# A gated cross-attention layer on one core: the loads of the split queries requested by SyncE in place of ScalarE, with other buffers and another front

## The reference

```
x = x + tanh(g_xattn) * xattn(layernorm(x), ctx)     # 16 heads of 32
x = x + tanh(g_ffn)   * ffn(layernorm(x))
xattn: q = x Wq + bq;  k = y Wk + bk;  v = y Wv + bv
       out = softmax(q k^T / sqrt(32)) v;  return out Wo + bo
ffn:   s = max(amax(|x|), 1e-6)/127;  x_q = clip(round(x / s))
       return (x_q @ weight_q^T) * s * weight_scale + bias
```

## Time and profile before

| what | before |
|---|---|
| median of 3 timed executions | 806.0 us (805.67 to 806.8) |
| the profiled execution: device time | 809.15 us |
| the profiled execution: span of the profile | 807.0 us |
| mean granted TensorE clock | 0.991 of full speed |
| busy: PE, PEld | 769.5 us (95%), 531.2 us (66%) |
| busy: DVE, ACT, POOL | 584.6 us (72%), 610.1 us (76%), 533.8 us (66%) |
| DMA | 183.21 MB, mean 227 GB/s |

### The profile page before, as it was taken

The page is one execution under the profiler, slowest core; times in us unless marked ns, Lnnn a source line. Parts: engine busy times, 40 slices in busy tenths (PEclk is TensorE's granted clock), DMA queues, the critical chain, the costliest instruction groups (busy, mean ns, idle before and its releaser), DMA issues.

```text
span 807.0 us, 16228 instructions
## 1 busy us (share of the span) xinstructions
PE 769.5 (95%) x5835; PEld 531.2 (66%) x5890; DVE 584.6 (72%) x879; ACT 610.1 (76%) x844; POOL 533.8 (66%) x524
## 2 busy tenths in 40 slices
PE   9896999999999999999999999999999989999996
PEld 6664467667666766766676676667667657666563
DVE  5864778677776857777686777768578796756568
ACT  5774668778687877868788786878778677787785
POOL 4836348485775948577595857759485765855588
PEclk9998999999999999999999999999999999999998
DMA  8899897879888887878878798788879757746722
GB/s 284 298 311 247 212 272 212 248 212 261 239 225 246 222 265 211 258 227 236 251 225 235 216 258 250 219 248 228 251 218 264 213 161 242 208 151 185 202 67 104
DMA packets 119519, 183.21 MB, mean 227 GB/s; under 512 B 37648, under 2 KB 47248, under 8 KB 117392
## 3 DMA queue, kind: packets, MB, share of 16 engines
q1 hardware_dynamic: 92368, 133.33, 54.2%
q10 hardware_dynamic: 27072, 48.84, 23.6%
HBM read 123.91 MB, written 58.22 MB: 226 GB/s over the span
## 4 chain that ended last, share of the span: by engine, by line
PE 75%; DVE 7%; DMA 6%; issue 5%; POOL 3%; ACT 3%; SPq 1%; ACTq 1%; DVEq 0%; POOLq 0%
PE bank_b L437 25%; PE bank_a L437 15%; PE scores L492 7%; PE scores L511 6%; PE sum_ps L519 6%; PE pv_ps L523 6%; PE bank_a L567 4%; DMA q_rows<-q_parts 2%; DVE row_max L1228 2%; PE scores L437 1%; PE bank_a L542 1%; PE bank_b L567 1%; DMA q_stack<-q_rows 1%; DMA x_in<-in_x 1%; SPq L232 1%
## 5 line engine op out<-in xcount | busy, mean ns | idle before, releaser
L1584 POOL TENSOR_TENSOR o_lo<-on,o_hi 128x512 fp32r<-128x512 f32 x48 | 64.6, 1346 | 135.9 <-ACT o_hi L907 135.9
L1228 DVE TENSOR_REDUCE row_max<-scores 128x16 f32<-128x1920 f32 x64 | 137.7, 2151 | 10.3 <-PE scores L492 10.3
L1239 DVE TENSOR_TENSOR q_parts<-q_sb,q_parts 128x512 fp32r<-128x512 f32 x60 | 64.3, 1072 | 111.4 <-ACT q_parts L851 111.4
L889 ACT ACTIVATE probs<-scores 120x2048 f32<-120x2048 f32 x64 | 120.0, 1876 | 18.8 <-PE scores L511 18.6
L1540 POOL TENSOR_TENSOR xt<-xt,rstd_b 128x512 f32<-128x512 f32 x60 | 97.8, 1665 | 6.8 <-DMA xt<-in_x_t 5.8
L492 PEld LDWEIGHTS scores<-k_sb,q_sb 32*128 32x128 f32 x1984 | 61.0, 186 | 51.9 <-issue 44.4
L1580 POOL TENSOR_TENSOR x<-x,gbo_r 128x512 f32<-128x512 f32 x64 | 93.6, 1474 | 0.6 <-DMA x<-in_x 0.5
L1592 POOL TENSOR_TENSOR x<-x,gbias_r 128x512 f32<-128x512 f32 x64 | 83.2, 1302 | 15.7 <-ACT cen L913 14.7
L511 PE MATMUL scores<-q_stack,k_stack 128*120 128x512 f32 x256 | 73.0, 406 | 12.5 <-DVE row_max L1228 8.7
L1597 POOL TENSOR_TENSOR x<-x,u_sb 128x512 f32<-128x512 f32 x56 | 74.2, 1324 | 7.1 <-DVE u_sb L1320 7.0
L437 PE MATMUL bank_b<-xt_hi,wq_hi 128*128 128x512 f32 x188 | 77.0, 409 | 1.2 <-DVE xt_lo L1218 1.2
(11 more groups left out here) (235 smaller groups left out, 1927.5 us busy)
## 6 DMA issues: line engine op xcount, KB each, us to landing
q_stack<-q_rows ACTq DMA_DIRECT2D x183, 256.0 KB, 4.3
q_rows<-q_parts SPq DMA_DIRECT2D x61, 512.0 KB, 4.5
xt<-in_x_t SPq DMA_DIRECT2D x16, 1024.0 KB, 8.7
x<-in_x SPq DMA_DIRECT2D x64, 256.0 KB, 4.2
out_x<-x SPq DMA_DIRECT2D x61, 256.0 KB, 2.3
x_in<-in_x SPq DMA_DIRECT2D x60, 256.0 KB, 5.1
k_stack<-k_rows SPq DMA_DIRECT2D x96, 120.0 KB, 4.4
k_rows<-k_parts SPq DMA_DIRECT2D x28, 240.0 KB, 2.2
```

Source lines behind the costliest of these rows:

```text
L889: act.activation(probs[0:KEYS], scores[0:KEYS], ACT.Exp, scale=SCALE).then_inc(p_ready, 1)
L1228: dve.tensor_reduce(row_max[:].rearrange("p (t r) j -> p r t j", r=ROWG)[:, :, :, j], scores[:, :, 0:QT * KEYS].rearrange("p r (t k) -> p ...
L1584: pool.tensor_tensor(o_lo[i % 2][j], on[:], o_hi[i % 2][j].bitcast(F32), ALU.subtract).then_inc(o_split, 1)
```

## The change

SP requests all `stack_q` loads; ACT requests none of them. `q_sb` becomes one buffer and `q_parts` two. DVE's `split_low` takes the query from the PSUM bank, adds the bias in the same instruction and subtracts the high part, so `q_sb` is free earlier, and the bank later: PE now waits for `q_split` before it writes a bank again. The low parts of the keys move from DVE to POOL. `split_high` waits for the store of two groups before. In step 0 SP requests the stack of group 3 and the store of the queries of batch 1, group 1, ahead of the loads for batch 2; in the front POOL and SP have another order, and ACT's conversion of the output weights stands behind `split_high(1, 1)`. At the end of step 14 the maxima are transposed ahead of the last chunk of an output projection. `max_sp` is stored with overlapping windows.

```diff
-        q_sb = [sb(f"q_sb{i}", [P, S]) for i in range(2)]
-        q_parts, k_parts = sb("q_parts", [P, 2, S], F32R), sb("k_parts", [P, 2, KEYS2], F32R)
+        q_sb = sb("q_sb", [P, S])
+        q_parts = [sb(f"q_parts{i}", [P, 2, S], F32R) for i in range(2)]
+        k_parts = sb("k_parts", [P, 2, KEYS2], F32R)
...
@@ block.sync @@
             store_rstd(2)
-            load_rstd(2)
-            load_xt(2)
 
             def step(i):
+                if i > 0:
+                    stack_q(i, 2)
                 if is_batch(e):
                     store(e, 0)
...
+                stack_q(i, 3)
                 if is_batch(e):
                     store(e, 1)
                 if is_batch(b):
                     store_q(b, 1)
                 if i == 0:
+                    load_rstd(2)
+                    load_xt(2)
                     load_x(f, 2)
...
+                if is_batch(b):
+                    stack_q(b, 0)
                 if is_batch(k_of(i)):
                     store_k(k_of(i) // 2, 2 * (i % 2))
...
+                if is_batch(b):
+                    stack_q(b, 1)
@@ block.tensor @@
                     pe.wait_ge(v_ready, nth(b, 1))
+                if keys_next or values_next and i > 1 or not is_batch(n):
+                    pe.wait_ge(q_split, nth(b - 1, DT, 0))
                 if is_batch(e):
                     quantised_layer(e, 1, bank_a if is_batch(n) else bank_b)
...
                     quantised_layer(e, 3, bank_b)
+                pe.wait_ge(q_split, nth(b - 1, DT, 2))
@@ block.scalar @@
             def split_high(n, j):
                 act.wait_ge(q_ready, nth(n, DT, j))
...
-                if n == 1 and j == 0:
-                    act.wait_ge(q_stored[0], stores_of(0, 0))
-                elif n > 0:
-                    act.wait_ge(q_stored[(j - 1) % DT], stores_of(n - (j == 0), (j - 1) % DT))
-                act.activation(q_parts_of(n, j)[0], q_of(n, j), ACT.Copy).then_inc(q_hi_done, 1)
-
-            def stack_q(n, j):
-                act.wait_ge(q_stored[j], stores_of(n, j))
-                act.wait_ge(s_done, nth(n, DT, j) - 2)
-                for block, part in enumerate((0, 1, 0)):
-                    load(q_stacked[j % 2], q_stack[j % 2][STRIPS[block]].bitcast(F32),
-                         q_rows[j, part].rearrange("(r d) s -> d r s", d=DH))
+                if n > 0 and j >= 2:
+                    act.wait_ge(q_stored[j - 2], stores_of(n))
+                if n == 1 and j < 2:
+                    act.wait_ge(q_stored[j], stores_of(0))
+                if n > 1 and j < 2:
+                    act.wait_ge(q_stored[j + 2], stores_of(n - 1))
+                act.activation(q_parts_of(n, j)[:, 0], q_of(n, j), ACT.Copy).then_inc(q_hi_done, 1)
@@ block.vector @@
-            def split_low(n, j):
+            def split_low(n, j, bank):
                 dve.wait_ge(q_hi_done, nth(n, DT, j))
-                dve.tensor_tensor(q_parts[:, 1], q_of(n, j), q_parts[:, 0].bitcast(F32), ALU.subtract).then_inc(q_split, 1)
+                parts = q_parts_of(n, j)
+                dve.scalar_tensor_tensor(out=parts[:, 1], in0=bank[:], scalar=bq_c[:, j:j + 1], in1=parts[:, 0].bitcast(F32),
+                                         op0=ALU.add, op1=ALU.subtract).then_inc(q_split, 1)
@@ block.gpsimd @@
                 if is_batch(e):
                     add_out(e, 2)
+                if is_batch(k_of(i)):
+                    low_k(k_of(i) // 2, 2 * (i % 2))
                 if is_batch(m):
                     x1_deviations(m, 0)
```

More of the change, by code:

```diff
@@ L202, in q_parts_of @@
         def q_parts_of(n, j):
[L203 to L206, removed]
+            return [o_lo1, o_hi1][j - 2][:, 0:2] if n == 0 and j >= 2 else q_parts[j % 2][:]
         def k_parts_of(pair, j):
@@ L278, in store_q @@
                     sp.wait_ge(q_stacked[j % 2], 48 * nth(n - 1, 2, j // 2))
[L279 to L284, removed]
+                sp.dma_start(q_rows[j].rearrange("h p s -> p h s"), q_parts_of(n, j).bitcast(F32)).then_inc(q_stored[j], 16)
             def stack_q(n, j):
-                sp.wait_ge(q_stored[j], stores_of(n, j))
+                sp.wait_ge(q_stored[j], stores_of(n))
                 if n > 0 or j >= 2:
@@ L294, in store_k @@
             def store_k(pair, j):
[L295 to L298, removed]
+                sp.wait_ge(k_split, nth(pair, DT, j))
                 if pair > 1:
@@ L335, in _ @@
             load_ctx(1)
+            store_k(0, 0)
+            store_q(0, 0)
             load_x(2, 0)
-            store_k(0, 0)
             store_k(0, 1)
-            store_q(0, 0)
+            stack_q(0, 0)
             load_x(2, 1)
             stack_k(0, 0)
-            stack_q(0, 0)
             store_q(0, 1)
+            load(rest_landed, u_sb[:].bitcast(I32), rows(wq8))
+            stack_q(0, 1)
+            load_x(2, 2)
+            store_q(0, 2)
+            load_x(2, 3)
             store_k(0, 2)
             store_k(0, 3)
[L346 to L349, removed]
             store_q(0, 3)
-            load_x(2, 2)
-            load_x(2, 3)
             load(rest_landed, gbo_r[:], bo.partition_broadcast(P))
@@ L499, in turn_max @@
                 for t in range(QT):
-                    ins = pe.matmul(bank[:, t * P:(t + 1) * P], max_sp[:, t], ident_r[:], start=True, stop=True)
+                    ins = pe.matmul(bank[:, t * P:(t + 1) * P], max_sp[:, t * DH:t * DH + P], ident_r[:], start=True, stop=True)
                 ins.then_inc(max_turned, 1)
@@ L679, in step @@
                     quantised_layer(m, 0, bank_a)
+                pe.wait_ge(q_split, nth(b - 1, DT, 3))
+                if is_batch(m) and i < LAST - 1:
                     project_o(m, 3, bank_b)
+                if i == LAST - 1:
+                    for c in range(DT - 1):
+                        add_heads(m, 3, c, bank_b)
                 if i == 0:
@@ L997, in step @@
                     split_high(b, 1)
-                stack_q(i, 3)
+                if i == 0:
+                    act.wait_ge(wo_gated, 1)
+                    act.activation(flat(wo_hi), flat(wo_stage), ACT.Copy).then_inc(wo_hi_done, 1)
                 log_sums(i, 1)
@@ L1336, in step @@
                 if is_batch(b):
-                    split_low(b, 0)
+                    split_low(b, 0, bank_b)
                 if is_batch(e):
@@ L1353, in step @@
                 if is_batch(b):
-                    split_low(b, 1)
+                    split_low(b, 1, bank_b)
                     maxima(b, 1)
@@ L1374, in step @@
                 if is_batch(b):
-                    split_low(b, 2)
+                    split_low(b, 2, bank_a)
                     maxima(b, 2)
```

88 lines of the change are left out of this document (43 added, 45 removed).

## The result

The changed kernel takes 817.06 us (median of 4 runs, 812.8 to 818.28) beside 806.4 for the kernel before on the same chip (805.67 to 807.0). The ratio, taken over the single executions and not from the two medians, is 1.0123, with a 95% interval of 1.0084 to 1.0162. Forecast were 795.5 us and a range of 789 to 803. The profiled execution takes 816.25 us, its span 814.6, beside 809.15 and 807.0.

The account below looks back on a forecast made before the run. PE was taken to bound the kernel from step 2 on, waits the front. From the median: 806.0 - 12.4 (front) + 3.6 (PE's new waits) - 1.1 (low part) - 0.6 (step 14) = 795.5 us; range 789 to 803.

Parts of the forecast that it names:

- The front's gains: Steps 0 and 1: 6.2 third quarter, 1.2 fourth, 2.3 first, 1.5 step 1, 1.2 shorter maxima waits; 12.4 us in all.
- The third quarter's 9.3 us: Step 0, third quarter: 9.3 us long instead of 15.44, 6.2 less, with bounds of 3 and 6.3.
- the first quarter's lower bound: Step 0, first quarter: gain of 0 instead of 2.3 us if the later keys' stack takes over PE's wait.
- I take 1.2, with 0 and 2.0 as bounds: Step 0, fourth quarter: 1.2 us gained from a higher granted clock after less idle time.
- The loads on SP: Middle steps: twelve more requests a step on SP cost 0, since each stack has about 23 us.
- The rival in which DMAs eat the front's gain: Step 0: busy DMA engines make stacks late; half the gain, 6.2 us, left; 801.7 us; chance 0.17.
- PE's new waits: First quarter of six even steps: 0.4 us each for DVE's split, 2.4; third quarter: 0.1 in 12 steps, 1.2.
- The 1.2 us for the keys' low part in the third quarter: Third quarter of 12 steps: POOL's keys' low part delays the deviations and DVE's split; 0.1 us each.
- The split on DVE: DVE's split reading a bank, a column and an SBUF tensor takes 0.74 us; bounds 0.67 and 1.94.
- The slower rival that hung on it: DVE's split is held up while POOL scales: 1.2 us more in 12 steps, 14.4; 810 us; chance 0.06.
- The 6.6 us of one low part on DVE: One keys' low part on DVE cost PE 2.2 us; moved to POOL, half counted as gain, 1.1 us.
- The end of step 14: Maxima transposed sooner shorten PE's 1.4 us wait for the last low part; 0.6 us gained, between 0 and 1.4.

Follow-up runs that it names:

- keys_first: Changed kernel with each step's first store of the keys' parts ahead of the stack of queries, in step 0 ahead of the factors' load; 805.41 us, 0.9958.
- both_moved: Changed kernel with the edits of keys_first and waits_moved together; 801.63 us, ratio 0.9931 to the kernel before.
- rows_first: both_moved with the loads of two rows of x for batch 3 ahead of the factors and xt in step 0; 802.05 us, 0.9935.
- keys_first_act: Changed kernel with the edits of keys_first and loads_act together; 807.34 us, ratio 0.9993 to the kernel before.
- after: The changed kernel itself, as described under the change; 817.06 us, ratio 1.0123 to the kernel before.
- loads_act: Changed kernel with the stacks of queries requested by ACT again, at the places of the kernel before; 812.42 us, ratio 1.0050.
- rows_first_act: rows_first with the stacks of queries requested by ACT; 804.08 us, ratio 0.9944 to the kernel before.
- before_on_sp: Kernel before with only the stacks of queries requested by SP, at their places in the changed kernel; 810.01 us, ratio 1.0018.
- waits_moved: Changed kernel with PE's wait for the first query split behind the quantised layer, POOL's first keys' low part behind x1's deviations; 812.58 us, 1.0053.

## Why the prediction was wrong, point by point

- **The front's gains** came, most of them: step 0 starts 1.7 us sooner and its first quarter is 1.0 shorter (2.7, forecast 2.3), the third quarter 4.7 (forecast 6.2), the first three quarters of step 1 3.0 (forecast 1.5 and a part of 1.2). That is 10.4 of the 11.2 that are left of the 12.4 without the fourth quarter's 1.2. The third quarter's 9.3 us were right where the clock was full: 9.17 in keys_first. In the changed kernel it ran at a mean clock of 0.84, behind a wait of 2.2 us for the stack of keys at the end of the second quarter; keys_first has the same wait there and a clock of 1.00, so why the clock fell in the one stays open. That wait is the one that the first quarter's lower bound named, one quarter later.
- **The step that failed** is "I take 1.2, with 0 and 2.0 as bounds" for the fourth quarter, together with step 1's fourth, for which no term stood: 8.4 and 6.3 us more. With them step 2 begins 5.2 us later, where the front was to give 12.4: 17.6 us apart, of 21.6 by which the median missed the forecast. The working looked for what holds step 1 and found `xt`, which came about when it had come before (requested at 66.03, scaled until 79.85). It did not follow the store of the keys' parts, which the change leaves in its place in SP's list while all around it moves. The trace of before showed it: requested at 70.58, 9.1 us on its way, landed at 79.7, and ACT copied the next high part at 79.88, one us ahead of the exponentials at 80.87:

```profile
70.58 0.73 SPq L301 DMA_DIRECT2D k_rows<-k_parts  x1
...
79.88 0.39 ACT L864 ACTIVATE k_parts<-k_sb 128x240 fp32r<-128x240 f32 x1
80.87 1.88 ACT L889 ACTIVATE probs<-scores 120x2048 f32<-120x2048 f32 x1 [0.60 <-PE scores L511]
```

The wait that was to be removed ended at 78.77 and hid a second one that ended 1 us later. Once the third quarter ended 6.5 us sooner, at 72.23 and not at 78.77, that store was what PE waited for. keys_first shows that this store was the cause, and also that it wasn't the only one: with the store early the fourth quarter still takes 18.90 us (21.55 in both_moved), behind the two rows of x and PE's new wait for the split. Only with these rows early as well, in rows_first, does it take 13.76. There step 1 begins at 85.06, where 81 to 83 were forecast, and step 2 at 133.16, 5.4 us sooner than before and not 12.4.
- **The loads on SP** cost nothing in a middle step, as forecast. "SP has only requests to make" was the wrong reason in the front: SP also waits, and what stands behind its waits and its loads is late. The rival in which DMAs eat the front's gain had the kind right, with 0.17, but named the stack of batch 1 for it and half of the gain; it was a store, and one and a half times the gain of 10.4 (15.6 us lost, with the second quarter's 0.8).
- **The rule of the rings.** With the requests 0.2 us apart, the first store of the keys in step 1 takes 10.8 us in keys_first and 6.6 in keys_first_act, where the stacks are on ACT's queue; after and loads_act give 10.7 and 7.4, rows_first and rows_first_act 10.2 and 9.1, before_on_sp and the kernel before 6.4 and 3.7. The Trainium skill, "DMA: Bandwidth & Descriptors", in "Queues, rings and completion order", would have it so: a transfer stands behind all that its own ring holds and takes turns with the other's. The traces agree there in direction, in all four pairs. The ring isn't all of it: both_moved has 5.2 with the stacks on SP. In step 0 the late store took 9.3 with the stacks on SP and 10.9 with them on ACT; `xt` and rows of x are on SP's queue in both.
- **PE's new waits** were right in kind and place and 0.2 short in size: 3.4 us in six even steps, 0.6 each, forecast 0.4. The one in step 0 was not counted; it cost nothing in the changed kernel and 7.3 us in both_moved. The 1.2 us for the keys' low part in the third quarter didn't come: no wait stands there, and that quarter takes 10.44 us in the changed kernel as in both_moved, where that part stands behind the deviations (10.39 before). Middle steps grew by 0.7 in even ones and 0.1 in odd ones. Of the 4.9 us (570.85 beside 568.34 less the 2.4 by which step 12 was too long in the trace of before), 3.7 go in both_moved (567.14). The other 1.2, some 0.1 a step, stay open.
- **The split on DVE** was right: 718 to 752 ns in all 60, and 731 at most in the 13 that ran while POOL scaled. The slower rival that hung on it did not come.
- **The 6.6 us of one low part on DVE** are no property of that place: before_on_sp, which still makes these parts on DVE, has a step 12 of 47.11 us, and its longest such part took 1.48. Nothing can be said of the half that was counted. **The end of step 14**: that step is 0.4 us shorter (44.67 before, 44.28 now), but PE's wait of 1.4 stays, and 0.1 is left at the end.

## What to carry to other kernels

Ahead of taking the longest wait for a gain, write down for each engine that passes that point when its next wait would end if the first were gone; a wait that ends one us later caps the gain. Then do the same for the next one: here the rows of x stood behind the store. A list of requests on one engine is a queue of waits as well: before adding loads to it, look at each store behind them and at who waits for its buffer. Where a bank or buffer gets a new wait, put it right ahead of the instruction that writes the bank, not at the head of the stretch.

## What the hardware showed unexpectedly

- The same 240 KB store took 2.1 to 4.9 us in step 0 when it was requested ahead of `xt` (the kernels with keys_first's edit), and 9.1 to 10.9 behind it (the others).
- The split that reads one operand from PSUM took 718 to 752 ns in 60 instructions, 43 of them with POOL at work in the same time. The one it replaces, with both operands in SBUF, took 0.67 to 1.94 us in steps 6 and 7. Which of the operands makes the difference wasn't tried by itself.
- Runs of one kernel spread by some 6 us (802.86 to 808.77 in keys_first), though from step 2 to the end of step 13 the executions of both_moved, rows_first and waits_moved agree within 0.4 us (567.14, 567.05, 567.45). In which stretch the spread lies, a single trace of each kernel can't show.
